# The quantised MLP stage of a fused attention and MLP kernel: factor of its second norm taken from the first norm's variance, the first tile's norms one step earlier, two places for weight codes

## What is computed

```
x = x + tanh(g_xattn) * xattn(layernorm(x), ctx)      # self attention, cross attention, relu MLP, three norms
x = x + tanh(g_ffn)   * ffn(layernorm(x))

ffn(x):  h = layernorm(x) * ln_gamma + ln_beta
         w1 = (fc1_q - 128) * scales  (512 x 2048)     w2 = (fc2_q - 128) * scales  (2048 x 512)
         return x + 0.5 * (silu(h @ w1 + fc1_bias) @ w2 + fc2_bias)
```

## Time and profile before

| | |
|---|---|
| median of 3 runs | 1837.16 us (1835.31 to 1838.54) |
| the profiled execution, its time | 1834.65 us |
| its span in the trace | 1832.8 us |
| TensorE matmuls busy | 1714.0 us (94%), 7838 of them |
| VectorE, ScalarE, GpSimd busy | 913.7, 531.2 and 328.3 us (50%, 29%, 18%) |
| mean granted clock of TensorE | 0.973 |

### The profile page before, as it was taken

One profiled execution on the slowest core, in us unless ns is written; L12 is line 12 of the kernel. 1 busy time (PEld: TensorE's weight loads), 2 busy tenths in 40 slices (PEclk: granted clock), 3 DMA queues, 4 the chain that ended last, 5 costly groups with the idle time before them and its releaser, 6 DMA issues.

```text
span 1832.8 us, 22184 instructions
## 1 busy us (share of the span) xinstructions
PE 1714.0 (94%) x7838; PEld 1385.4 (76%) x7838; DVE 913.7 (50%) x1810; ACT 531.2 (29%) x933; POOL 328.3 (18%) x500
## 2 busy tenths in 40 slices
PE   6797999997989999889999979999999999999999
PEld 5586788875777888667777757787878787878787
DVE  3465654446466545456767776634343434343411
ACT  3231212112212111246556533322222222222222
POOL 0111110002011001035566652000000000000000
PEclk9799999998989999979999989999999999999999
DMA  4211211113021111444444423210101010101000
GB/s 133 103 53 36 80 35 52 35 34 104 26 63 59 46 35 35 129 155 147 149 143 152 149 86 133 61 43 1 47 1 46 1 46 1 46 1 46 1 24 23
DMA packets 68870, 117.38 MB, mean 64 GB/s; under 512 B 11233, under 2 KB 13281, under 8 KB 68603
## 3 DMA queue, kind: packets, MB, share of 16 engines
q1 hardware_dynamic: 64013, 108.34, 18.2%
q10 hardware_dynamic: 4744, 7.58, 1.3%
HBM read 81.05 MB, written 34.84 MB: 63 GB/s over the span
## 4 chain that ended last, share of the span: by engine, by line
PE 84%; DVE 9%; issue 2%; ACT 2%; DMA 1%; POOL 1%; DVEq 0%; SPq 0%; ACTq 0%; POOLq 0%
PE banks L582 78%; PE banks L592 3%; PE banks L706 2%; DVE split_q L1361 1%; DVE small L1667 1%; DVE split L1361 1%; ACT split_q L933 1%; PE banks L793 1%; DVE plain L1416 1%; DVE split L1827 1%; ACT split L933 1%; DVE plain L1854 1%; DVE small L1410 0%; DMA plain<-in_x 0%; DMA plain<-in_L_xattn_Wk 0%
## 5 line engine op out<-in xcount | busy, mean ns | idle before, releaser
L582 PE MATMUL banks<-split 128*128 128x512 f32 (+4 forms) x2292 | 558.1, 394 | 42.6 <-DVE split L1361 24.1
L582 PE MATMUL banks<-split_q,split 128*128 128x512 f32 x2304 | 572.3, 398 | 4.4 <-DVE split_q L1458 4.4
L582 PEld LDWEIGHTS banks<-split 128*128 128x128 f32 (+3 forms) x2292 | 420.7, 190 | 150.0 <-DVE split L1361 26.8
L582 PEld LDWEIGHTS banks<-split_q,split 128*128 128x128 f32 x2304 | 431.2, 190 | 103.1 <-issue 15.2
L582 PE MATMUL banks<-split,split_q 128*128 128x512 f32 (+3 forms) x1824 | 419.9, 384 | 7.5 <-DVE split_q L1361 3.0
L582 PEld LDWEIGHTS banks<-split,split_q 128*128 128x128 f32 x1824 | 329.2, 192 | 67.7 <-issue 5.6
L1361 DVE TENSOR_TENSOR split<-banks,split 128x512 fp32r<-128x512 f32 (+5 forms) x234 | 148.9, 641 | 189.9 <-ACT split L933 189.2
L1231 POOL TENSOR_TENSOR small<-small 128x1 f32<-128x1 f32 (+1 forms) x104 | 29.5, 283 | 1167.9 <-DVE small L1412 595.2
L933 ACT ACTIVATE split<-banks 128x512 fp32r<-128x512 f32 (+5 forms) x234 | 126.4, 557 | 363.4 <-PE banks L706 229.7
L1827 DVE TENSOR_TENSOR split<-plain,split 128x512 fp32r<-128x512 f32 x128 | 89.2, 697 | 226.5 <-ACT split L1202 226.5
L1196 ACT ACTIVATE plain<-banks,small 128x512 f32<-128x512 f32 x128 | 88.0, 687 | 301.9 <-PE banks L582 301.9
(11 more groups left out here) (142 smaller groups left out, 1173.3 us busy)
## 6 DMA issues: line engine op xcount, KB each, us to landing
plain<-in_x SPq DMA_DIRECT2D x56, 256.0 KB, 3.0
xo_scratch<-plain SPq DMA_DIRECT2D x32, 256.0 KB, 3.3
x_scratch<-plain SPq DMA_DIRECT2D x32, 256.0 KB, 2.0
plain<-x_scratch SPq DMA_DIRECT2D x32, 256.0 KB, 2.9
tile_x<-xo_scratch SPq DMA_DIRECT2D x32, 256.0 KB, 3.1
xg_scratch<-tile_x SPq DMA_DIRECT2D x32, 256.0 KB, 2.0
out<-plain SPq DMA_DIRECT2D x32, 256.0 KB, 2.1
tile_x<-x_scratch SPq DMA_DIRECT2D x28, 256.0 KB, 4.5
```

What stands on the lines that cost most here:

```text
L582: mm = nc.tensor.matmul(out, left(c, l), right(c, r), start=start and c == 0 and (l, r) == PASSES[0], stop=stop and c == chunks - 1 and (l ...
```

## The change

- **Factor of the second norm.** The mean of h0 is zero and its variance is v * r^2, so its root is (v * r^2 + eps)^-0.5. GpSimd works out r and r times that root for four blocks at once, from v alone, in seven instructions in a chain (`roots_of_x`). `make_h0`, its statistics and its two GpSimd instructions for each block are gone. `h_scale` is one instruction from x, `h_shift` one.
- **Residual on ScalarE.** x + gate * h0 is x * (1 + gate * r) - gate * m * r: two small instructions of VectorE for four blocks (`make_factors`) and one of ScalarE for each block (`base_x`). In stage 3 VectorE still adds the bias, right behind `lo_h`.
- **One step earlier.** `stats_x3` for tile 0 stands in `step2(6)` behind `add_z(7, 3)`, ahead of `add_y(6, 0)`; the norms of its first two blocks stand at the start of `last_step`, ahead of the rest of tile 6.
- **Two places for codes.** Units 1, 3, ... 15 use `q1_odd`, `sc1_odd`, and a unit is loaded when the last but one is done. W1 is finished first: step 6 takes units 12 to 15 (all of W1's last rows), the last step two (the first two of W2). The loads of ln_gamma, ln_beta and fc2_bias wait for the probabilities of tile 7 and no longer for its norms.

```diff
         q1, sc1 = codes1[:, 0], codes1[:, 1]
+        q1_odd, sc1_odd = plain(4096, E), plain(4608, E)
...
-            return w2_unit(n - 14) if n in (14, 15) else w1_unit(n - (12 if n < 14 else 14), 3)
+            return w1_unit(n - 12, 3) if n < 16 else w2_unit(n - 16)
...
             def load_unit(n):
-                if n:
-                    sp.wait_ge(w_ready, n)
+                q, sc, done, _ = unit_stage(n)
+                if n > 1:
+                    sp.wait_ge(w_ready, n - 1 if n < 17 else n)
...
                 elif t + 2 == NT:
-                    sp.wait_ge(x2_ready, NT * BT)
+                    sp.wait_ge(tp_free, 2 + probs_at(NT - 1) + 1)
...
-                load_unit(2 * t + 2)
+                load_unit(2 * t + 3)
+                if t + 2 == NT:
+                    load_unit(2 * t + 4)
                 if t + 1 == NT:
-                    sp.wait_ge(hn_ready, BT)
+                    sp.wait_ge(base_made, BT)
...
+            def base_x(t, slot, k, x):
+                act.wait_ge(base_factors, 2 * t + 2)
+                act.wait_ge(x3_scaled, t * BT + k + 1)
+                nc.scalar.activation(base[:, slot, k], x, ACT.Identity, bias=baseM[:, k:k + 1],
+                                     scale=baseS[:, k:k + 1]).then_inc(base_made, 1)
...
                 if ahead:
-                    hi_w(2 * t, q1, unit(2 * t))
+                    hi_unit(2 * t)
+                else:
+                    act.wait_ge(xg_ready, t * BT)
+                    base_x(0, 0, 0, x1b[:, 0])
                 relu(t, 3)
...
+            def roots_of_x(t):
+                var, eps, root_ = mvX[:, :, 1], eps_col.to_broadcast([P, BT]), half.to_broadcast([P, BT])
+                pool.wait_ge(var_ready, R3 + t + 1)
+                p2.link(nc.gpsimd.tensor_tensor(rs_x, var, eps, ALU.add))
+                p2.link(nc.gpsimd.tensor_tensor(rs_x, rs_x, root_, ALU.pow))
+                p2.link(nc.gpsimd.tensor_tensor(rsH, var, rs_x, ALU.mult))
+                p2.link(nc.gpsimd.tensor_tensor(rsH, rsH, rs_x, ALU.mult))
+                p2.link(nc.gpsimd.tensor_tensor(rsH, rsH, eps, ALU.add))
+                p2.link(nc.gpsimd.tensor_tensor(rsH, rsH, root_, ALU.pow))
+                nc.gpsimd.tensor_tensor(rsH, rsH, rs_x, ALU.mult).then_inc(x3_factors, 1)
...
                 lo_hid(t, 3)
+                if t + 2 == NT:
+                    lo_w(2 * t + 1)
                 for k in range(BT):
                     root_z(t + 1, k)
+                if t + 2 == NT:
+                    roots_of_x(0)
                 root_y(t, 0)
-                lo_w(2 * t + 1)
+                lo_w(2 * t + 1 if t + 2 < NT else 2 * t + 2)
...
             def last_step(t, kept):
                 add_y(t - 1, 3)
+                dve.wait_ge(x3_factors, 1)
+                make_factors(0)
+                dve.wait_ge(vec3_in, 32)
+                dve.wait_ge(w_ready, NT * 2)
+                h_scale(0, 0, x1b[:, 0])
+                h_scale(0, 1, x1b[:, 1])
+                h_shift(0, 0)
+                h_shift(0, 1)
                 shift_y(t - 1, 2, kept)
...
-            def make_h0(steps, t, k, x):
+            def h_scale(t, k, x):
                 dve.wait_ge(tp_full, t * BT + TP3 + max(k - 1, 0))
-                return steps.done(nc.vector.tensor_scalar(H0[:, k % 2], x, mvX[:, k, 0:1],
-                                                          rs_x[:, k:k + 1], ALU.subtract, ALU.mult))
+                nc.vector.scalar_tensor_tensor(out=H0[:, k % 2], in0=x, scalar=mvX[:, k, 0:1], in1=vec3[:, 0],
+                                               op0=ALU.subtract, op1=ALU.mult).then_inc(x3_scaled, 1)
...
                         if f in TURN_AT:
-                            lo_h(t + 1, 1 - slot, TURN_AT.index(f))
+                            k = TURN_AT.index(f)
+                            x = base[:, 1 - slot, k]
+                            lo_h(t + 1, 1 - slot, k)
+                            dve.wait_ge(base_made, (t + 1) * BT + k + 1)
+                            nc.vector.tensor_tensor(x, x, bias3, ALU.add).then_inc(bias_added, 1)
```

More of the change, by code:

```diff
@@ L1208, in tile3 @@
                         hi_h(t + 1, 1 - slot, TURN_AT.index(f))
+                    if f + 1 in TURN_AT and not last:
+                        k = TURN_AT.index(f + 1)
+                        base_x(t + 1, 1 - slot, k, base[:, 1 - slot, k])
             tiles(tile3)
@@ L1740, in step2 @@
                 scale_w(2 * t)
+                if not far:
+                    scale_w(2 * t + 1)
                 lo_probs(t + 1)
```

188 lines of the change are left out of this document (78 added, 110 removed).

## The result

The changed kernel takes **1819.19 us** (median of 4 runs, 1816.11 to 1820.83), the kernel before 1836.29 us beside it (4 runs, 1835.31 to 1838.54). The ratio is 0.9898, 95% interval 0.9882 to 0.9913: 17.1 us faster, where 22 were forecast. The sign, the range (1810 to 1824) and the places were right; the size was not quite. The profiled execution took 1819.9 us, its span is 1818.1 us, 14.7 us under that of before.

The account below looks back on a forecast made before the run. TensorE, busy 94% of the span, was taken as the bound, with gains only at its waits and lower clock. The transition's 17.0 us plus the turns' 5.3 made 22.3 us off 1837.2, giving 1815 us, range 1810 to 1824.

Parts of the forecast that it names:

- (1): End of stage 2: tile 0's statistics run earlier, so the 2.00 us wait before `mlp_in(7, 1)` goes; later `add_y(6, 0)` is hidden.
- (2): Step 6: more codes work on VectorE and GpSimd, unit 15 landing at 1043; `mlp_in(7, 0)` waits 0.7 us, a new cost.
- rival A: VectorE becomes the bound of the last two steps, by GpSimd collisions or late unit 15: 1818 to 1823 us; chance 0.17.
- (3): Last step: tile 0's first two blocks are done by 1056.5, so the 2.28 us wait of `turn_h(0, 0)` goes.
- (4): Last step: `turn_h(0, 2)` waits 1.8 us for `h_shift(2)`, `mlp_out(7, 0)` 0.1 us; new cost 1.9 us.
- (5): Last step takes two units instead of four; the 2.42 us wait of `ffn_out(1)` and the 0.57 go.
- The sum of the stretch: From stage 2 to stage 3: 19.6 us winnable, less 0.7 and 1.9, gives 17.0 us; bounds 9.8 to 19.6.
- Turns: Stage 3: `lo_h` to `lo_hid3` falls from 2.13 to 1.88 us, winning 0.25 us at each of 21 turns, 5.3 us.
- Rival B: Stage 3 turns do not shrink: the bias holds `lo_hid3` or the instruction pair costs 2.1 us; 1820 us; chance 0.08.
- Factor chain: Stage 3: seven GpSimd instructions between statistics and `h_scale(0)` take 3.6 us, hidden, costing nothing.
- Rival C: Slower: in each of 7 tiles VectorE waits for the factor chain, hurting from 8.1 us on; 1846 us; chance 0.03.
- Rival D: No change: the waits only move and the turns give less than 4 us; 1833 to 1837 us; chance 0.04.

Follow-up runs that it names:

- AFTER: The changed kernel itself, with the whole change applied to the kernel before and none of the follow-up edits: 1819.19 us, ratio 0.9898.

## Why the prediction was right, and where its sizes were off

**(1) Statistics.** Right. The 2.00 us wait is gone, and the run with the statistics at their old place brings 2.03 us back. What it called hidden costs 1.0 us in the step, as the runs with and without them show: not by the length of the statistics, but by a collision that the factor chain brings about. What else those two runs lose is not split between the statistics and the chain, which moved together.

**(2) Units 13 to 15.** The mechanism was named and its size was the largest error: 2.7 us for 0.7. It shows as waits of 0.52 and 1.46 us at two groups of transposes ahead of `mlp_in(7, 0)`, and not in front of it. The landing of unit 15's scales was put at 1043 in the time of before; it was 1046.96 - 2.8 (the shift of the profiled run) = 1044.2. And the list was counted at the durations of instructions alone, without the collision with GpSimd (1.57 for 0.74) that rival A priced in the same text. Rival A, given 0.17, is the nearest to this: both of its conditions were met in part (one collision on the path where it counted four, the scales 1.2 us late and not 3), at 2.0 us instead of 3 to 5. The measured 1819.19 us lies in its band, 1818 to 1823, and not in the forecast's own, 1811 to 1818, which was given 0.68. The stated range holds because it took both in.

**(3) First two blocks.** Right: no wait at either turn; the cover was enough.

**(4) Last two blocks.** The wait had its size, 1.48 us and 0.28 for a forecast of 1.8 and 0.1. The step that failed is the sentence that the waits found "are shorter than those after which the clock fell". The clock did fall: from `mlp_out(7, 1)` to `mlp_out(7, 2)` it took 5.36 us where 3.80 are needed at the full clock, 1.6 us more. "PEclk 1.00 in all windows" was wrong, by the text's own test. The bound had such a stretch in it, the sum had not.

**(5) Units 16, 17.** Right: the 2.42 us and the 0.57 are gone, and they stay away with one place for the last units too. What that run pays is in step 6, which takes the units that the last step no longer has. That the second place makes this free the prediction took for granted; the run shows that it carries 16 us.

**The sum of the stretch.** Forecast 17.0 us, measured 12.45 + 2.7 - 2.7 = 12.5. Of the missing 4.5 us, 2.0 are in (2), 1.6 the clock, and 0.5 in `mlp_out(7, 0)`, which takes 3.9 us without its two waits where 3.37 were reckoned. About 0.9 more is the floor: 31.2 us was too low. Against that, `ffn_out(1)` won 0.3 more than forecast and the waits of (4) were 0.1 shorter. A turn was taken at 0.35 us, and two with nothing between them and the next block take 0.97 (1066.66 to 1067.63); the four `mlp_in` take 11.3 and not 10.9.

**Turns.** Forecast 0.25 us each and 5.3 in all; measured 0.22 and 4.6 to 5.0. Rival B falls. The bound of 15.8 us "if the wait goes wholly" was excluded for this change rightly, and one moved instruction brought 12.8 of it.

**Factor chain.** Right: 3.5 us for a forecast of 3.6, hidden, and still hidden at 7.8 us. Rival C falls. Rival D falls with the result.

The medians came nearer to the forecast (17.1 of 22.3) than the profiled pair did (14.7), because the profiled execution of AFTER had lost 2.8 us before the change begins. A sum made against one profiled execution carries such variation on both sides.

## What to carry to other kernels

When an engine's list is shortened, ask at each wait which instruction directly ahead of the late one could stand behind it: the change took 66 us of work from VectorE and won 5 us at the turns, and moving one 0.68 us addition won 12.8. Count the collision of VectorE and GpSimd into every sum in which both are busy, and before a pass is moved away from one victim look at who is its next neighbour: a move that shortened one VectorE instruction by 1 us, and no stretch by anything, cost 4 to 5 us behind it. A second place for a transfer is worth pricing by itself, for it may be what makes a new order free.
